# Column maxima of the attention scores from differences and relu on TensorE, with negated odd keys

## The reference

```python
# B, S, D, H = 8, 512, 256, 16; DK = D // H
q = (layernorm(x) @ Wq + bq).reshape(B, S, H, DK)
k = (ctx @ Wk + bk).reshape(B, S, H, DK)
v = (ctx @ Wv + bv).reshape(B, S, H, DK)
scores = einsum('bqhd,bkhd->hbqk', q, k) / sqrt(DK)
attn = softmax(scores.reshape(H * B, S, S), axis=0)      # over all 128 (head, batch)
x = x + tanh(g_xattn) * (einsum('hbqk,bkhd->bqhd', attn, v) @ Wo + bo)
x = x + tanh(g_ffn) * ffn(layernorm(x))                  # fake-quantised gate, up, down
```

## Time and profile before

| | us |
|---|---|
| median of 3 runs (847.61 to 850.77) | 848.94 |
| the profiled execution | 855.71 |
| its span, first to last instruction | 853.6 |
| the first stage, to the first matmul of the maxima | 130.2 |
| the maxima, to the first matmul of the attention | 184.8 |
| the attention, to about | 690 |

### The profile page before, as it was taken

The page is one execution under the profiler, slowest core; times in us unless marked ns, Lnnn a source line. Parts: engine busy times, 40 slices in busy tenths (PEclk is TensorE's granted clock), DMA queues, the critical chain, the costliest instruction groups (busy, mean ns, idle before and its releaser), DMA issues. The chain is left out here.

```text
span 853.6 us, 20038 instructions
## 1 busy us (share of the span) xinstructions
PE 740.9 (87%) x8129; PEld 447.5 (52%) x8151; DVE 757.1 (89%) x825; ACT 680.9 (80%) x1094; POOL 474.8 (56%) x225
## 2 busy tenths in 40 slices
PE   8897897777777769999999999999999999559977
PEld 6564372111212225677666777677777677424334
DVE  4799646999999978999999999999999995758957
ACT  3444448999999979899998999999999834759873
POOL 1233454000000000999999999999999997415500
PEclk9999998999999989999999999999999999879989
DMA  9897798766766627668867787868867794000014
GB/s 294 276 305 225 218 276 208 197 174 172 194 175 174 239 91 235 186 185 281 264 190 206 236 291 212 225 197 288 260 194 213 242 312 138 0 1 1 1 50 147
DMA packets 98442, 165.87 MB, mean 194 GB/s; under 512 B 9712, under 2 KB 37104, under 8 KB 98032
## 3 DMA queue, kind: packets, MB, share of 16 engines
q1 hardware_dynamic: 98352, 164.60, 64.3%
HBM read 134.42 MB, written 42.73 MB: 208 GB/s over the span
## 5 line engine op out<-in xcount | busy, mean ns | idle before, releaser
L1011 POOL TENSOR_TENSOR e<-e,recip 128x1792 f32<-128x1792 f32 (+3 forms) x128 | 367.9, 2919 | 19.3 <-DVE recip L1042 19.2
L963 ACT ACTIVATE e<-psY 128x512 f32<-128x512 f32 x512 | 296.3, 646 | 33.7 <-PE psY L896 28.2
L1029 DVE TENSOR_REDUCE partial<-e 128x128 f32<-128x4096 f32 (+1 forms) x80 | 283.3, 3559 | 7.2 <-ACT e L963 7.2
L896 PE MATMUL psY<-arena 128*128 128x128 bf16 x2048 | 200.6, 221 | 1.8 <-DMA arena<-k_stack 1.7
L896 PEld LDWEIGHTS psY<-arena 128*128 128x128 bf16 x2048 | 149.3, 98 | 75.8 <-issue 26.1
L699 ACT ACTIVATE copies<-ps_max 128x1024 bf16<-128x1024 f32 x189 | 175.9, 1045 | 0.6 <-PE ps_max L678 0.6
L892 PE MATMUL psY<-shift,minus 128*128 128x512 bf16 x396 | 153.1, 387 | 10.9 <-PEq L633 5.5
L715 DVE TENSOR_TENSOR high<-copies,high 128x3072 bf16<-128x3072 bf16 x63 | 109.8, 1744 | 0.0
L1002 POOL MEMSET ones_w<- 96x128 bf16 x1 | 0.2, 206 | 174.0 <-POOLq L633 174.0
L912 PE MATMUL psX<-e,arena 128*32 128x128 f32 x2048 | 76.2, 288 | 3.0 <-issue 1.3
L296 POOL TENSOR_TENSOR parts<-rest,parts 128x512 bf16<-128x512 f32 x32 | 37.5, 1177 | 73.7 <-ACT parts L440 73.6
(11 more groups left out here) (170 smaller groups left out, 1005.8 us busy)
## 6 DMA issues: line engine op xcount, KB each, us to landing
arena<-k_stack SPq DMA_DIRECT2D x256, 256.0 KB, 3.3
arena<-q_stack SPq DMA_DIRECT2D x64, 256.0 KB, 4.4
k_stack<-parts SPq DMA_DIRECT2D x40, 256.0 KB, 3.6
q_stack<-parts SPq DMA_DIRECT2D x40, 256.0 KB, 3.5
arena<-in_x_dram SPq DMA_DIRECT2D x8, 1024.0 KB, 10.8
k_stack<-k_stack SPq DMA_DIRECT2D x12, 512.0 KB, 11.4
arena<-in_ctx_dram SPq DMA_DIRECT2D x4, 1024.0 KB, 6.7
arena<-q_stack SPq DMA_DIRECT2D x8, 512.0 KB, 8.2
```

The source lines that it names most:

```text
L896: last = nc.tensor.matmul(bank[:, j * P:(j + 1) * P], ks[:, i % KRING, b * P:(b + 1) * P], qs[:, h, b * P:(b + 1) * P], start=False, stop= ...
L963: nc.scalar.activation(e_at(p, half * HB, (half + 1) * HB).rearrange("p q z i -> p z q i"), ps[n % SCORES][:].rearrange("p (z q i) -> p z ...
L1011: nc.gpsimd.tensor_tensor(part, part, by_pairs(recip[:, r % 2, :], share), ALU.mult).then_inc(pool_scaled, 1)
L1029: nc.vector.tensor_reduce(partial[:, :, k, :], e[:, t:t + n].rearrange("p t q z i -> p q i t z"), AX.XY, ALU.add).then_inc(sum_done, 1)
```

## The change

A round g is now one couple of heads and one batch, again 64 rounds. The odd heads' keys are negative in the stack: their projection weights are permuted with scale -1 (two instructions in place of one) and their biases multiplied by a sign tile. Both heads' keys share one tile, one half each, with no zeros. For chunks 0 to 2, a matmul over all 128 rows gives the difference even minus odd (X, into `ps_x`); ScalarE writes its relu as bf16 (`gain`); TensorE then adds the negated odd score (64 rows) and `minus` times `gain` (128 rows) in `ps_y` (Y), which is minus the larger of the two; VectorE takes the minimum with `lowest` straight from PSUM, chunk 0 alone and chunks 1 and 2 together. For chunk 3 two matmuls of 64 rows, one on the upper and one on the lower half of the rows, give both heads' scores in two banks (C, `ps_c`); ScalarE copies them, and every second round VectorE takes a maximum of the even and a minimum of the odd ones in bf16, 128x1024 each. Three small instructions at the end fold chunk 3. `shift` becomes `lowest`, the negated maximum: attention adds it with `plus` (an identity) for even heads and subtracts it for odd ones, and the odd heads' exponential has a negative scale. The zero halves, their memsets, and the `zero_w` tile go; the first couple's odd keys are loaded in `prepare` with the rest.

```diff
# prepare
-                            load_pair(sp, 0, k_stack, q_stack, keep["k_first"], None, keep["q_first"],
+                            load_pair(sp, 0, k_stack, q_stack, keep["k_first"], keep["k_first"], keep["q_first"],
                                       keep["first_loaded"])
...
-                pool.wait_ge(s["transposed"], TR * (NC - 1))
                 pool.wait_ge(s["part3_ready"], NC * UN)
-                pool.memset(keep["k_first"][HALF:P], 0.0).then_inc(s["k_zeroed"], 1)
...
+                    for j, value in enumerate(signs):
+                        last = nc.scalar.activation(
+                            w_p[:].rearrange("p c (e d h) -> p (c e) d h", e=DC, d=DK)[:, :, :, j::step],
+                            w_s[:].rearrange("p c (e h d) -> p (c e) d h", e=DC, d=DK)[:, :, :, j::step],
+                            ACT.Copy, scale=value)
...
                 act.wait_ge(s["b_loaded"], 16 * 2 * DC)
+                act.wait_ge(s["bias_signed"], 1)
...
                 normalise(0)
+                dve.wait_ge(s["id_f"], 2)
+                nc.vector.tensor_reduce(sign[:, 0:1], ident[:, 1:P:2], AX.X, ALU.max).then_inc(s["sign_set"], 1)
...
+                nc.vector.tensor_scalar(bk_s[:], bk_s[:], sign[:, 1:2], None, ALU.mult).then_inc(s["bias_signed"], 1)
# maxima, TensorE
+                def differences(g):
...
+                    for kc in range(MIXED):
+                        if g:
+                            pe.wait_ge(gained, 2 * (g - 1) + (2 if kc == MIXED - 1 else 1))
+                        nc.tensor.matmul(ps_x[:, kc, :], keys(g, kc, slice(0, P)), queries(g, slice(0, P)),
+                                         start=True, stop=True).then_inc(x_scored, 1)
+                def plain(g):
...
+                        pe.wait_ge(c_copied, g)
+                    for j, rows in enumerate((EVEN, ODD)):
+                        last_mm = nc.tensor.matmul(ps_c[:, j, :], keys(g, MIXED, rows), queries(g, rows),
+                                                   start=True, stop=True)
...
+                def smaller(g):
+                    for kc in range(MIXED):
+                        if g:
+                            pe.wait_ge(y_merged, 2 * (g - 1) + (1 if kc == 0 else 2))
+                        nc.tensor.matmul(ps_y[:, kc, :], keys(g, kc, ODD), queries(g, ODD), start=True, stop=False)
+                        pe.wait_ge(gained, 2 * g + (2 if kc == MIXED - 1 else 1))
+                        nc.tensor.matmul(ps_y[:, kc, :], minus[:], gain[:, g % RING, kc, :], start=False, stop=True
+                                         ).then_inc(y_scored, 1)
+                for g in range(GROUPS):
+                    differences(g)
+                    plain(g)
+                    if g:
+                        smaller(g - 1)
+                smaller(GROUPS - 1)
# maxima, ScalarE
+                    for k0, k1 in ((0, MIXED - 1), (MIXED - 1, MIXED)):
+                        act.wait_ge(x_scored, MIXED * g + k1)
+                        nc.scalar.activation(gain[:, g % RING, k0:k1, :], ps_x[:, k0:k1, :], ACT.Relu
+                                             ).then_inc(gained, 1)
+                    act.wait_ge(c_scored, g + 1)
...
+                    nc.scalar.activation(dst, ps_c[:], ACT.Copy).then_inc(c_copied, 1)
# maxima, VectorE
+                    for n, (k0, k1) in enumerate(((0, 1), (1, MIXED))):
+                        dve.wait_ge(y_scored, MIXED * g + k1)
...
+                            nc.vector.tensor_tensor(lowest[:, k0:k1, :], ps_y[:, k0:k1, :], lowest[:, k0:k1, :], ALU.min
+                                                    ).then_inc(y_merged, 1)
...
+                    if g > 2 and g % 2:
...
+                        for j, op in enumerate((ALU.max, ALU.min)):
...
+                            nc.vector.tensor_tensor(last[:, j], copies[:, m % RING, j], last[:, j], op
+                                                    ).then_inc(c_merged, 1)
...
+                for j, op in enumerate((ALU.max, ALU.min)):
+                    nc.vector.tensor_tensor(folds[:, j, :], last[:, j, 0, :], last[:, j, 1, :], op).then_inc(c_merged, 1)
+                dve.wait_ge(c_merged, merges + 2)
+                nc.vector.scalar_tensor_tensor(out=lowest[:, MIXED, :], in0=folds[:, 0, :], scalar=-1.0, in1=folds[:, 1, :],
+                                               op0=ALU.mult, op1=ALU.min).then_inc(folded, 1)
# attend
-                        nc.tensor.matmul(bank[:], minus[:], shift_at(qc, kc).to_broadcast([P, HB, P]),
+                        nc.tensor.matmul(bank[:], (plus, minus)[h % 2][:], shift_at(qc, kc).to_broadcast([P, HB, P]),
...
-                                ACT.Exp, scale=DK ** -0.5).then_inc(exped, 1)
+                                ACT.Exp, scale=(DK ** -0.5, -DK ** -0.5)[half // 2]).then_inc(exped, 1)
```

More of the change, by code:

```diff
@@ L134, in prepare @@
         ident = sb("ident", [P, P])
-        ident_b = sb("ident_b", [P, P], BF16)
+        ident_b = keep["plus"]
+        sign = sb("sign", [P, 2])
         diag = sb("diag", [P, DC, P])
@@ L602, in maxima @@
 def maxima(nc, sem, k_stack, q_stack, keep):
[L611 to L614, removed]
+    lowest, plus, minus = keep["lowest"], keep["plus"], keep["minus"]
     RING = 2
-    COPIED = NC - 1
+    MIXED = NC - 1
     COUPLES = H // 2
+    GROUPS = COUPLES * B
+    EVEN, ODD = slice(0, HALF), slice(HALF, P)
     with ExitStack() as es:
@@ L620, in head_tile @@
             return es.enter_context(nc.sbuf_tensor(name, [P, NC, CT], BF16))
[L622 to L625, removed]
-        spare = es.enter_context(nc.sbuf_tensor("spare_exp", [P, 1], F32))
[L627 to L631, removed]
+        k_pair = [keep["k_first"], head_tile("k_pair1")]
+        q_pair = [keep["q_first"], head_tile("q_pair1")]
+        gain = es.enter_context(nc.sbuf_tensor("gain", [P, RING, MIXED, S], BF16))
+        copies = es.enter_context(nc.sbuf_tensor("copies", [P, RING, 2, 2, S], BF16))
+        last = es.enter_context(nc.sbuf_tensor("last", [P, 2, 2, S], BF16))
+        folds = es.enter_context(nc.sbuf_tensor("folds", [P, 2, S], BF16))
+        spare = es.enter_context(nc.sbuf_tensor("spare_exp", [P, 1], F32))
+        ps_x = es.enter_context(nc.psum_tensor("ps_x", [P, MIXED, S], F32))
+        ps_y = es.enter_context(nc.psum_tensor("ps_y", [P, MIXED, S], F32))
+        ps_c = es.enter_context(nc.psum_tensor("ps_c", [P, 2, S], F32))
+        loaded = [keep["first_loaded"], sem("pair_loaded1")]
+        x_scored, c_scored, y_scored, gained, c_copied, y_merged, c_merged, folded = (
+            sem("max_" + n) for n in ("x_scored", "c_scored", "y_scored", "gained", "c_copied", "y_merged", "c_merged",
+                                      "folded"))
         with nc.Block() as block:
@@ L635, in _ @@
             def _(sp):
-                for p in range(COUPLES):
+                for p in range(1, COUPLES):
                     if p >= 2:
[L638 to L644, removed]
+                        sp.wait_ge(y_scored, MIXED * B * (p - 1))
+                    load_pair(sp, p, k_stack, q_stack, k_pair[p % 2], k_pair[p % 2], q_pair[p % 2], loaded[p % 2])
+                    for what in STACK_COPIES[COPIES_A_COUPLE * (p - 1):COPIES_A_COUPLE * p]:
+                        copy_rows(sp, k_stack, q_stack, what, keep["k_copied"], keep["q_copied"])
                 sp.dma_start(keep["wT_dram"], keep["wT"][:]).then_inc(keep["wT_saved"], 16)
@@ L658, in _ @@
             def _(pe):
[L659 to L672, removed]
-                            pe.wait_ge(direct, g)
-                        elif g:
-                            pe.wait_ge(copied, g * COPIED + (kc + 1 - COPIED))
-                        for j in range(LANES):
-                            b = bp * LANES + j
-                            last = nc.tensor.matmul(
-                                ps[:, kc, j * S:(j + 1) * S], k_head[:, kc, b * P:(b + 1) * P],
-                                q_both[p % 2].rearrange("p c (b q) -> p c b q", q=P)[:, :, b, :], start=True, stop=True)
-                        last.then_inc(scored, 1)
@@ new lines, in keys @@
+                def keys(g, kc, rows):
+                    return k_pair[g // B % 2][rows, kc, g % B * P:(g % B + 1) * P]
+                def differences(g):
+                    p = g // B
+                    if g % B == 0:
+                        pe.wait_ge(loaded[p % 2], 16 * COUPLE_PIECES * (p // 2 + 1))
+                    for kc in range(MIXED):
[3 more added lines that the diff above has]
+                                         start=True, stop=True).then_inc(x_scored, 1)
@@ L800, in attend @@
         recip = sb("recip", [P, 2, P])
-        minus, zero_w = keep["minus"], keep["zero_w"]
+        plus, minus, zero_w = keep["plus"], keep["minus"], keep["zero_w"]
         banks = [keep["psX"][:, 0, :], keep["psX"][:, 1, :]] + [keep["psY"][:, i, :] for i in range(SCORES + 2)]
```

86 lines of the change are left out of this document (40 added, 46 removed).

## The result

| | before | changed |
|---|---|---|
| first comparison, median us (runs) | 849.71 (4) | 859.32 (4) |
| second comparison, median us (runs) | 852.61 (19) | 862.21 (8) |
| ratio, first | | 1.009 (1.0061 to 1.0119) |
| ratio, second | | 1.010 (1.0068 to 1.0132) |
| span of the profiled execution, us | 853.6 | 858.2 |

The kernel became about 1% slower, 8 to 10 us, where +4.2 us, 853.1, was forecast: the direction was right and the size less than half of it. 859.3 lies above the forecast's own 850 to 857 and inside the 8-in-10 range of 842 to 865. The profiled execution of before (855.71) lay 6 us above that kernel's median and the one of after (860.02) 0.7 us above its own, so their spans differ by only 4.6 us.

What follows compares the result with a forecast made beforehand. VectorE was taken to set the 2.80 us round, ScalarE just behind, TensorE with slack. Terms of +0.2, +1.5 and +2.5 gave +4.2 us, 853.1 us; own range 850 to 857, 8-in-10 range 842 to 865.

Steps and rivals of the forecast that it cites:

- The round: Maxima: VectorE and TensorE wait for each other, two rounds take 5.59 us, 2.80 a round, as before the change.
- both legs of the loop: Maxima, two rounds: 2.65 us from the 1024-column minimum's start through TensorE's Y matmuls, then 2.94 of VectorE work.
- the change of shape: TensorE in the maxima: each switch between 64-row and 128-row matmuls costs 0.10 us, six a round, 0.60.
- TensorE's own sum: TensorE's work in a maxima round: 10 x 0.215 + 0.60 = 2.75 us.
- the first rival: Maxima: switching matmul rows costs nothing beside 512 columns or is hidden; a round 2.65, 842.4 us in all; chance 0.22.
- the two C matmuls run side by side: Chunk 3 in the maxima: using different row halves and banks, they overlap and save TensorE the whole 0.215 us.
- two rivals: Maxima: switching matmul rows is free (842.4 us, chance 0.22); the C matmuls do not overlap (863.5 us, chance 0.22).
- The tail: End of the maxima: merges, folds and waits after the last minimum take 2.74 us, so +1.5 (bounds +0.8 and +2.2).
- The load ahead of the last writes: End of the first stage: 512 KB more in the queue before the last query writes, +2.5 us.
- the start of the maxima: First rounds: matmuls of double length for the first 4 us, an estimate, make 1 us of the result.
- The sum: Whole kernel: +0.2 for the maxima's rounds, +1.5 after the last minimum, +2.5 in the first stage, +4.2 us.
- The start of the first stage: First key output delayed 4.5 us by the biases' sign, delay gone by the third key output: 0 (bound 1.4).

Runs made afterwards that it cites:

- e6: Changed kernel with only the two chunk-3 matmuls made full ones of 128 rows: 872.44 us, ratio 1.0227 to the kernel before.
- e7: Changed kernel with one chunk-3 merge in every round in place of two in every second: 860.06 us, ratio 1.0088 to the kernel before.
- e5: Changed kernel with every 64-row matmul of the maxima made a full one of 128 rows: 847.67 us, ratio 0.9943 to the kernel before.
- e9: Changed kernel with Y's odd part as a full matmul on zero-padded odd keys, merges unchanged: 849.56 us, ratio 0.9958 to the kernel before.
- e3: Kernel before with only the load of the first couple's odd keys moved ahead of the first stage's last writes: 855.44 us, ratio 1.0032.
- e4: Changed kernel with 20 matmuls of no use at the end of the first stage: 859.55 us, ratio 1.0086 to the kernel before.

## Why the prediction was right, and where it was not

**The round** was right in its mechanism. 2.80 was forecast and measured, with both legs of the loop; the change of shape, taken as 0.10 from 256-column matmuls, is 0.107 beside 512-column ones (e6, e7), which puts TensorE's own sum at 2.79 where 2.75 was forecast, only 0.01 below the loop; without the change of shape the loop is 2.65 as the first rival's working had it (e5, e9); the two C matmuls run side by side, and losing that costs 0.20 (e6), forecast 0.16. ScalarE's relu of 1024 columns costs what a copy does, 0.92 us for 0.93. So two rivals had their arithmetic right and their condition wrong. With 512 columns no run hid the cost; the Trainium skill's rule that a change of tiling mode drains TensorE (TensorEngine Tiling (Array Packing), Key Properties) agrees with the 0.107. The C rows and e6 show the two row halves working in parallel; the Trainium skill's statements that different tiles can execute in parallel (same page, Key Properties) and that they must not use the same bank (Restrictions and Gotchas) agree with the 0.23 us to the next start.

**The tail** was right: 2.72 us from the last minimum's end, forecast 2.74.

**The load ahead of the last writes** was right by the timing (+2.7, 1.1 to 4.3, for +2.5), and SyncE's wait grew by 1.2 to 2.0. The maxima's first matmul, however, was to be at about 132.7, and no trace without the 20 matmuls has it so late: 131.55 in e3, and 129.1 to 131.8, in the mean 130.9, in the seven of the changed kernel and its variants, against 130.2 and 130.5. What takes the rest up is not settled.

**The step that failed in size** is the start of the maxima, "matmuls of double length for the first 4 us ... it makes 1 us of the result". No row gives the 4 us; the trace of before had 6.0 us at half speed at that place. In the changed kernel half speed lasted 9.4 us in the first trace and cost 3.0 us, 5.5 us in the second and cost 1.3 (both against e4), and 14.8 us in e7. In the first trace the clock also fell at the end, where TensorE waits for VectorE, and cost 0.8, a term that the forecast does not have. At full speed the maxima lasted 186.2 us (e4), where the forecast without its 1 us is 183.3 - 1 + 2.74 + 0.46 = 185.5; where that 0.7 comes from is open.

In the kernel before, about 6 us at half speed cost 1.3 to 1.4 (184.8 and 184.7 with it, 183.4 and 183.4 without), and the forecast set its changed kernel against a trace that held this. For the same length at half speed the two kernels thus pay alike, 1.3 for 5.5 us and 1.4 for 6.0; the changed kernel lost more where half speed lasted longer. That it lasts longer because the change took TensorE's slack is not shown: the changed kernel and its variants without the 20 matmuls had 3.8 to 14.8 us of it in seven traces, the kernel before and e3's variant 0 to 6.0 in three.

**The sum** in the traces' terms: maxima +4.6 in place of +1.7 (+1.5 of it the tail, and at full speed in both kernels +2.8 in all), first stage +0.5 by the mean start above, or +2.7 by e3's timing, in place of +2.5, together +5.1 to +7.3, where the times say 8 to 10. One to five us are open. Part of it is that the traced executions of before were long ones: the two traced executions of before took 6.0 and 2.8 us more than the medians beside them, those of the changed kernel 0.7 more and 0.4 less. Which stage an execution of before at the median passes faster, no trace shows. The stages after the maxima are 539.1 and 541.1 long after and 538.6 and 539.4 before, which could hold about 1 of it but is not clear of the spread from trace to trace (537.4 to 541.1 over all runs).

**The start of the first stage** cost nothing, as argued: the third key output was on time.

## What to carry to other kernels

Count a TensorE stream by its changes of shape as well as by its columns: here six changes of 0.107 us a round, with the two merges in every second round, took back all that the lighter VectorE and ScalarE work had given, and padding with zeros to full rows, the thing the change had removed, was the faster way. Two 64-row matmuls side by side save one matmul, 0.215 us, and when they stand alone among full ones their two changes of shape cost as much, 0.214 (an estimate from these runs; none had that as its limit). And when two limits lie close (a loop at 2.80, an engine at 2.79), an edit that lifts the loop alone shows nothing (e7); only both edits gave the 0.39 us a round.

## What the runs showed of the hardware

- A change between matmuls of 64 and of 128 contraction rows costs 0.107 us beside 512 columns, hardly more than the 0.10 beside 256: it does not shrink with longer matmuls.
- Two 64-row matmuls of 512 columns on different halves of the rows, into different banks, started so close that the next followed 0.23 us after the first.
- After a change of shape the weight load started only 0.01 us before its matmul, and 0.21 us before it where the shape stayed the same.
- After 3.9 to 5.0 us without a matmul the changed kernel spent 9.4, 5.5 and (with another order on VectorE) 14.8 us at the 1.2 GHz level, all with TensorE nearly always busy. In the first two this cost 3.0 and 1.3 us; in the kernel before, after 2.2 us without a matmul, 6.0 us at that level cost 1.4.
